# Sixteen-head attention: replicating the split queries and keys in six DMAs a batch instead of twelve

## What is computed

```
qkv = qkv.reshape(B, S, 3, H, D).transpose(2, 0, 3, 1, 4)     # H = 16 heads, D = 8
bias = jnp.minimum(rel[None, :, :] * slopes[:, None, None], MAX_BIAS)
scores = jnp.einsum('bhqd,bhkd->bhqk', q, k) * D ** (-0.5) + bias[None]
probs = jax.nn.softmax(scores, axis=-1)
out = jnp.einsum('bhqk,bhkd->bhqd', probs, v)
```

## Time and profile before

| What | us |
|---|---|
| median of three runs | 988.57 |
| the three runs | 988.5 to 989.13 |
| the profiled execution's own time | 988.53 |
| its span in the trace | 986.5 |
| TensorE busy in the span | 783.2 |

### The profile page before, as it was taken

The page is one execution under the profiler, slowest core; times in us unless marked ns, Lnnn a source line. Parts: engine busy times, 40 slices in busy tenths (PEclk is TensorE's granted clock), DMA queues, the critical chain, the costliest instruction groups (busy, mean ns, idle before and its releaser), DMA issues.

```text
span 986.5 us, 19021 instructions
## 1 busy us (share of the span) xinstructions
PE 783.2 (79%) x5641; PEld 564.8 (57%) x5641; DVE 549.3 (56%) x2190; ACT 395.9 (40%) x947; POOL 357.9 (36%) x543
## 2 busy tenths in 40 slices
PE   0798479999999999952489999999999982038894
PEld 0676355555666677742246676667666651028883
DVE  4688573233322332333588989898987714026672
ACT  0456121222212322210036666766676661025562
POOL 5000517777850134433222423242322102744552
PEclk9999668999999999986569999999999995559997
DMA  9970001111100132303654444444443014111110
GB/s 250 155 221 0 0 1 36 40 41 41 44 0 14 52 112 78 96 30 90 128 106 95 90 108 93 102 83 106 95 85 67 3 45 155 54 53 55 50 50 14
DMA packets 75114, 72.44 MB, mean 73 GB/s; under 512 B 8125, under 2 KB 65680, under 8 KB 72732
## 3 DMA queue, kind: packets, MB, share of 16 engines
q1 hardware_dynamic: 69436, 60.38, 27.3%
q0 software_dynamic: 5600, 11.12, 3.5%
HBM read 43.71 MB, written 27.33 MB: 72 GB/s over the span
## 4 chain that ended last, share of the span: by engine, by line
PE 52%; DVE 18%; issue 12%; DMA 5%; POOL 5%; ACT 3%; DVEq 2%; SPq 2%; POOLq 0%; ACTq 0%
PE bank L1475 10%; PE bank L1476 9%; DVE rt L1065 6%; PE bank L1498 6%; PE bank L1527 4%; PE bank L1617 3%; PE bank L1569 3%; POOL sorted_rows L766 3%; PE bank L1604 3%; PE bank L1599 2%; DMA arena<-arena 2%; SPq L548 1%; DVEq L1180 1%; PE bank L1435 1%; PE bank L1707 1%
## 5 line engine op out<-in xcount | busy, mean ns | idle before, releaser
L1065 DVE CUSTOM_DVE_ANT_0 rt<-bank,alibi 128x256 f32<-128x256 f32 x512 | 192.9, 419 | 44.4 <-PE bank L1569 37.5
L973 DVE TENSOR_TENSOR arena<-arena,bank 128x512 f32<-128x512 f32 (+1 forms) x128 | 75.0, 587 | 187.8 <-ACT arena L1253 187.8
L1280 ACT ACTIVATE arena<-bank 128x512 f32<-128x512 f32 x256 | 150.6, 598 | 55.4 <-PE bank L1604 49.5
L1253 ACT ACTIVATE arena<-bank 128x512 f32<-128x512 f32 (+1 forms) x128 | 66.1, 517 | 202.9 <-PE bank L1476 202.9
L1569 PE MATMUL bank<-arena 72*128 72x256 bf16 x512 | 104.7, 289 | 26.6 <-DMA arena<-qk_parts 13.4
L1599 PE MATMUL bank<-arena 81*128 81x256 bf16 x512 | 117.0, 274 | 8.3 <-ACT arena L1280 4.7
L1475 PE MATMUL bank<-arena 128*128 128x320 f32 (+2 forms) x256 | 115.7, 534 | 7.5 <-DVE arena L973 7.5
L1476 PE MATMUL bank<-arena 128*128 128x320 f32 (+2 forms) x256 | 111.9, 519 | 0.0
L1604 PE MATMUL bank<-arena,ident_b 128*128 128x256 bf16 (+8 forms) x544 | 80.2, 243 | 0.0
L1569 PEld LDWEIGHTS bank<-arena 72*128 72x128 bf16 x512 | 39.0, 102 | 69.4 <-DVE arena L1065 42.8
L1475 PEld LDWEIGHTS bank<-arena 128*128 128x128 f32 x256 | 42.8, 193 | 53.5 <-DVE arena L973 41.1
(11 more groups left out here) (242 smaller groups left out, 1402.9 us busy)
## 6 DMA issues: line engine op xcount, KB each, us to landing
arena<-qk_parts SPq DMA_DIRECT2D x48, 192.0 KB
arena<-qk_parts SPq DMA_DIRECT2D x144, 64.0 KB
qk_parts<-arena SPq DMA_DIRECT2D x16, 384.0 KB, 2.8
back_rows<-empty_row SPq DMA_DIRECT2D x1, 4096.0 KB, 37.8
arena<-back_rows SPq DMA_DIRECT2D x16, 256.0 KB, 3.8
arena<-in_w SPq DMA_DIRECT2D x2, 2048.0 KB, 10.9
xg_rows<-empty_row SPq DMA_DIRECT2D x1, 2580.0 KB, 38.5
arena<-xg_rows SPq DMA_DIRECT2D x8, 322.5 KB, 4.0
```

Source lines behind the costliest of these rows:

```text
L973: nc.vector.tensor_tensor(out, sil[:, k, 0:out.shape[1]], bank[4 + k][:, 0:out.shape[1]], ALU.mult).then_inc(hid_done, 1)
L1065: last = nc.vector.tensor_tensor_reduce(biased[n % 2 * QT + u], bank[n % 2][:, SEQ * u:SEQ * u + SEQ], alibi[:, h, P * (1 - u):P * (1 - u) ...
L1253: nc.scalar.activation(sil[:, k, 0:width], bank[2 + k][:, 0:width], ACT.Silu).then_inc(sil_done, 1)
L1280: nc.scalar.activation(prT3[:, n % (2 * HG)].rearrange("p k t -> p (k t)"), bank[2 + n % 2][:], ACT.Exp).then_inc(exp3_done, 1)
```

## The change

The three key loads of 24 rows become one load of 72 rows, whose source is read three times by a leading dimension of step 0. The nine query loads of 8 rows become four of 16 rows and one of 8: of the blocks 0 to 8 two neighbours go together; where both hold the same part (blocks 0 and 1, 4 and 5, 6 and 7) the source has a leading dimension of step 0 with 2 copies of 8 rows, where they don't (2 and 3) it is 16 rows in a row, and the last block goes alone. The counts that are waited for go from 192 to 96.

```
-            for a in range(PARTS):
-                r = PARTS * HD * a
-                sp.dma_start(ks[r:r + PARTS * HD, c % RING], rows[1]).then_inc(qk3_in[c % RING], 16)
-                for k in range(PARTS):
-                    sp.dma_start(qs[r + HD * k:r + HD * k + HD, c % RING], rows[0, HD * a:HD * a + HD]).then_inc(qk3_in[c % RING], 16)
+            sp.dma_start(ks[0:KROWS, c % RING], rows[1].unsqueeze(0).to_broadcast([PARTS, PARTS * HD, NH, SEQ])).then_inc(qk3_in[c % RING], 16)
+            for b in range(0, PARTS * PARTS, 2):
+                first, last = b // PARTS, min(b + 1, PARTS * PARTS - 1) // PARTS
+                n = min(2, PARTS * PARTS - b)
+                src = rows[0, HD * first:HD * first + HD * n] if last > first else rows[0, HD * first:HD * first + HD].unsqueeze(0).to_broadcast([n, HD, NH, SEQ])
+                sp.dma_start(qs[HD * b:HD * (b + n), c % RING], src).then_inc(qk3_in[c % RING], 16)
```

More of the change, by code:

```diff
@@ L515, in replicate @@
         def replicate(c):
-            wait_apart(sp, (parts_done, c + 1), *([(qk3_in[(c - 2) % RING], 192 * ((c - 2) // RING + 1))] if c >= 2 else []))
+            wait_apart(sp, (parts_done, c + 1), *([(qk3_in[(c - 2) % RING], 96 * ((c - 2) // RING + 1))] if c >= 2 else []))
             sp.dma_start(part_dram[c % 2].rearrange("w a p t -> p (w a) t"), part.rearrange("p w a t -> p (w a) t")).then_inc(parts_out[c % 2], 16)
@@ L1564, in score @@
             if h == 0:
-                pe.wait_ge(qk3_in[c % RING], 192 * (c // RING + 1))
+                pe.wait_ge(qk3_in[c % RING], 96 * (c // RING + 1))
             if n >= 2:
```

## The result

The changed kernel takes 1054.98 us against 988.54 us, medians of six runs each: ratio 1.0678 (95% interval 1.0644 to 1.0711), 66 us slower. Forecast were 1031 us, 43 us slower, with a range of 1008 to 1072. The direction and the places were right, and the pattern in part; the size was half as large again.

What follows compares the result with a forecast made beforehand. TensorE, nearly full and in order, was taken as the bound, with late DMAs paid almost fully. First scores, batch 1 and first maxima (14.4 us), plus steady batches (30), less 2, gave 42.4 us more: 1031 us, range 1008 to 1072.

Steps and rivals of the forecast that it cites:

- Confinement by the leading count: Replication loads: the smaller leading dimension sets the DMA engines, so the busiest two engines carry 50 rows, 16.0 us.
- Time of one replication: Replication loads on SP's queue: 18.1 us instead of 13.9, made of 16.0 data, 1.7 fixed and 0.4 slower first issue.
- First scores: Start of the sixteen-head stage: batch 0's first scores wait longer for the replicated rows, +4.2 us.
- Batch 1: Scores of batch 1: its parts' store queues behind the first replication, so its rows come late, +2.0 us.
- First maxima: Batch 0's transposed scores: maxima land behind batch 2's loads, a wait of 9.0 us, 8.2 more than before.
- Steady batches: Transposed scores of batches 1 to 13: maxima come late behind a replication, 2.3 us a batch on average, 30 us.
- The halving: Steady batches: a wait shortens the next without delaying the next replication, so 4.6 us lateness costs 2.3 a batch.
- the full price: Rival, steady batches: each wait puts off the next replication, 13 x 4.6 = 60 us instead of 30; 1061 us, chance 0.12.
- The clock: TensorE's half clock after long waits in the steady part: counted as nothing, at most 14 us.
- the second term: Transposed scores: `send_max` queues on SP behind the replication, so the maxima take 18.5 us instead of 13.9.
- The rival on the other side: Replication loads: unlike sides don't confine them and they run wider than before; 981 us, chance 0.06.
- The 37 rows: Replication loads: the rival on the other side decides once the busiest engine has fewer than 37 rows.

Runs made afterwards that it cites:

- the alike results with 32 and 33 rows: Changed kernel with three plain key loads again (32 rows on the busiest engine), ratio 1.0182; with nine plain query loads again (33 rows), 1.0197.
- the fill: Changed kernel with 26 idle matmuls ahead of the wait for the maxima in batches 1 to 13: ratio 1.0603; same edit on the kernel before: 1.0302.

## Why the prediction was right, and where its size came from

- **Confinement by the leading count**, which the prediction took from the constant rows: shown, by the share of 0.18, by the 3 and then 2 rows in flight, by the alike results with 32 and 33 rows, and by 12 rows in flight with the same 72 rows and no copies. The rule of the Trainium skill that the prediction names (DMA: Bandwidth & Descriptors, Why a DMA increments its semaphore by 16 and not by 1) agrees with these.
- **Time of one replication**, 18.1 us forecast, 20.3 measured. The rate was if anything too low: alone on its engine, a row takes 0.309 us (26.5 GB/s), and I used 25.6. What the term left out is, by the times of the pieces, the crowd at its start: while the load of 16 rows, `load_given` and the store of the next parts are in flight too, the rows take up to 0.8 us each. No run took these apart. The data phase was 17.8 us and not 16.0; before and behind it stand 2.1 us from the issue to the first piece and 0.4 to the first score, 2.5 where 2.1 were forecast.
- **First scores**: +4.2 forecast, +6.6 measured. **Batch 1**: +2.0 forecast, 4.6 measured. **First maxima**: 9.0 forecast, 10.4 measured. The three are 1.4 to 2.6 us above the forecast, about the 2.2 us by which the replication itself was longer.
- **Steady batches**: 30 us forecast, 46.6 - 10.4 = 36.2 measured. The halving was right: the full price, 13 times the measured lateness of a replication of 20.3 - 13.9 = 6.4 us, would be 83 us, and half of it is 42. That the waits came by turns holds from batch 6 on alone.
- **The clock**, left at nothing, was the other term that was mis-sized, beside the replication's length. Between the first scores and the last batch's, 477 to 794 us before and 484 to 862 us after, the matmuls' busy time is:

```profile
477.00:794.00 317.00, 296.66 (x2888) 204.61 (x2889) 269.60 (x1380) 199.26 (x422) 86.47 (x135) 0.95 0.42 87
```

```profile
484.00:862.00 378.00, 311.06 (x2890) 212.24 (x2891) 270.54 (x1381) 199.45 (x422) 86.38 (x135) 0.89 0.22 72
```

  14.4 us more for the same matmuls. I had argued that slower matmuls shorten the next wait. The bound that I gave for the case that they don't, 14 us, is what was measured, and the way it was reached fits as well: 13.6 of the 14.4 us fall behind 549 us, and seven stretches at half clock (1.2 GHz of 2.4) stand there, each during or just behind a wait of 2 us or more. How much of the 14 us the kernel would gain by full clock alone is open. In the traces the way from the first score to the last transposed one takes 392.3 us in the changed kernel and 382.5 with the fill; these 9.8 us less are 36.4 of fill put in, 31.9 of waits and 14.2 of clock taken out.
- **Sum**: 6.6 + 4.6 + 10.4 + 36.2 - 2.8 is 55.0 us of waits, 14.4 us of clock, and -1.8 us of TensorE's waits for VectorE (11.9 before, 10.1 after): 67.6 us. With the first loads going out 0.75 us later (464.18 against 463.43) that is 1.3 us above the 67.1 us between the spans.
- **The mechanism of the second term was incomplete.** "`send_max` stands in SP's queue behind the loads" explains the kernels as they are, but it is not what makes the maxima late: on ScalarE's queue they were as late (46.5 us of waits against 46.6). The times of the pieces above say that the load goes to the engines that carry the replication, and those are full.
- **The rival on the other side** had a true kernel: the loads before are held up, and wider plain loads gain 5 us. The change as made could not reach it. The 37 rows that the prediction gave as the turning point were wrong: with 32 and 33 rows on the busiest engine the kernel was still 2% slower, and its replication ends with 2.0 or 3.0 rows in flight.

## What to carry to other kernels

Before merging loads with a broadcast source, look at the leading dimension of both sides: fewer DMAs can mean fewer engines, and the busiest engine's bytes set the time. Store the copies, or order the blocks so that a plain wide load serves. A small load that others wait for can be as late as the busiest engine it shares: ScalarE's queue did not help here, and GpSimd's helped in part. And where one engine is full and another waits once a batch, a lateness costs by the chain: work out whether a wait puts off its own cause, since that halved the price here.

## What the runs showed that was not expected

Two queues on one engine seem to be served piece by piece: pieces of 512 B that take 0.027 us each passed at one in about 0.33 us beside rows of 8 KB. So a load of many small pieces suffers much; 24 KB took 9.7 us. And 36 us of idle work made the changed kernel no slower, if anything 4 to 7 us faster, while the clock stayed at 1.00 where it was 0.94.
